# Row-maximum scores as three fp32r products of split queries and keys, and output weights loaded once per batch

## What is computed

```python
q = shape(query_states @ wq, T)          # B=8, T=128, D=512, 16 heads of 32
k = shape(key_value_states @ wk, S)      # S=2048
v = shape(key_value_states @ wv, S)
scores = jnp.einsum('bhtd,bhsd->bhts', q, k) + bias
weights = jax.nn.softmax(scores, axis=-1)
attn = jnp.einsum('bhts,bhsd->bhtd', weights, v)
attn = jnp.transpose(attn, (0, 2, 1, 3)).reshape(B, T, D)
x = x + attn @ wo
```

## Time and profile before

| | |
|---|---|
| median of 3 runs | 2052.88 us (2052.06 to 2055.56) |
| the profiled execution | 2055.39 us, of which 2053.6 us lie between its first and last instruction |
| PE busy | 1886.2 us, 92% of the span, 17102 matmul instructions |
| PEld, weight loads | 1431.3 us, 70% |
| DVE, ACT, POOL busy | 1130.7, 777.9, 804.0 us |
| mean granted TensorE clock | 0.959 of full speed |

### The profile page before, as it was taken

The page is one execution under the profiler, slowest core; times in us unless marked ns, Lnnn a source line. Parts: engine busy times, 40 slices in busy tenths (PEclk is TensorE's granted clock), DMA queues, the critical chain, the costliest instruction groups (busy, mean ns, idle before and its releaser), DMA issues. The chain is left out here.

```text
span 2053.6 us, 40698 instructions
## 1 busy us (share of the span) xinstructions
PE 1886.2 (92%) x17102; PEld 1431.3 (70%) x17102; DVE 1130.7 (55%) x2160; ACT 777.9 (38%) x1295; POOL 804.0 (39%) x641
## 2 busy tenths in 40 slices
PE   7599999999999999999999999579879998599995
PEld 3477777677677677677677777367657877499995
DVE  4244656656656556657556557464765233455553
ACT  1233434344344434344344334241244130355552
POOL 0114677668668677667667662000000000100001
PEclk9899999999999999999999999789989997699998
DMA  8622121121121122122122101210041004799993
GB/s 166 209 88 87 53 73 56 54 79 58 48 78 58 52 73 63 47 76 70 38 78 68 35 30 33 90 52 14 1 139 31 1 1 173 281 368 358 359 359 110
DMA packets 101126, 210.82 MB, mean 103 GB/s; under 512 B 9088, under 2 KB 33968, under 8 KB 95840
## 3 DMA queue, kind: packets, MB, share of 16 engines
q1 hardware_dynamic: 99488, 204.02, 29.4%
q0 software_dynamic: 1472, 4.40, 0.7%
HBM read 187.68 MB, written 20.71 MB: 101 GB/s over the span
## 5 line engine op out<-in xcount | busy, mean ns | idle before, releaser
L369 POOL TENSOR_TENSOR total<-total,probT 128x512 f32<-128x512 f32 x392 | 502.7, 1282 | 231.6 <-ACT probT L411 207.5
L488 DVE TENSOR_REDUCE negm<-bank 128x1 f32<-128x512 f32 x512 | 326.8, 685 | 179.4 <-PE bank L572 175.0
L469 DVE TENSOR_TENSOR probT<-bank,shift 128x512 f32<-128x512 f32 (+1 forms) x512 | 291.2, 615 | 216.2 <-PE bank L584 216.2
L411 ACT ACTIVATE probT<-probT 128x1024 f32<-128x1024 f32 x256 | 271.2, 1060 | 227.4 <-DVE probT L469 214.6
L405 ACT ACTIVATE v<-bank 128x512 f32<-128x512 f32 x128 | 76.4, 597 | 478.3 <-PE bank L552 478.3
L345 POOL TENSOR_TENSOR ctx_lo<-ctx_raw,ctx_hi 128x512 fp32r<-128x512 f32 x128 | 165.7, 1295 | 153.2 <-ACT ctx_hi L391 148.9
L552 PE MATMUL bank<-ctx_hi,wkv_hi 128*128 128x512 f32 x512 | 152.1, 419 | 22.5 <-ACT ctx_hi L391 22.5
L602 PEld LDWEIGHTS bank<-probT,v 128*32 128x32 f32 x4096 | 104.0, 109 | 94.0 <-ACT probT L411 92.0
L584 PEld LDWEIGHTS bank<-q,k 32*128 32x128 f32 x4096 | 126.0, 186 | 46.5 <-issue 44.1
L1348 POOL MEMSET zero_sb<- 128x512 f32 x1 | 0.5, 525 | 393.2 <-POOLq L1118 393.2
L552 PE MATMUL bank<-wkv_hi,ctx_hi 128*128 128x512 f32 x512 | 152.6, 420 | 0.0
(11 more groups left out here) (236 smaller groups left out, 2800.8 us busy)
## 6 DMA issues: line engine op xcount, KB each, us to landing
w_sb<-w SPq DMA_DIRECT2D x10, 4096.0 KB, 14.2
w_sb<-w SPq DMA_DIRECT2D x40, 1024.0 KB, 6.3
ctx_raw<-ctxT SPq DMA_DIRECT2D x128, 256.0 KB, 3.2
bias<-bias_scratch SPq DMA_DIRECT2D x32, 512.0 KB, 5.3
shift<-turned_bias SPq DMA_DIRECT2D x32, 512.0 KB, 5.1
slots<-zero_sb SPq DMA_DIRECT2D x17, 256.0 KB, 3.0
bias_scratch<-btab SPq DMA_DIRECT2D x1, 3072.0 KB, 34.2
down_w<-down SPq DMA_DIRECT2D x11, 256.0 KB, 2.6
```

Of the source, the lines that this page charges most:

```text
L369: pool.tensor_tensor(total[:, g], total[:, g], part, ALU.add).then_inc(add_step, 1)
L411: act.activation(pT[:, u % 2, j:j + 2], pT[:, u % 2, j:j + 2], ACT.Exp).then_inc(exp_done, 1)
L469: dve.tensor_tensor(pT[:, u % 2, j, i0:], sc[:, i0:], shift[:, g, j].unsqueeze(1).broadcast_to([P, ST - i0, T]), ALU.add).then_inc(shifted, 1)
L488: dve.tensor_reduce(negm[:, c, h:h + 1], sc[:], AX.X, ALU.max, negate=True).then_inc(max_done, 1)
```

## The change

The scores of `scores(a)` are made of three fp32r products instead of one fp32 product: queries and keys are split into a rounded high part and the rest, and high times high, low times high and high times low are accumulated in the same PSUM bank. The three products form three rounds over the four strips. All four ring banks are waited for before the first round. ACT makes the high part of the keys by a second copy out of `kv_bank`, after the plain copy and after a wait for the scores of the step before (one buffer); `kv_out` is signalled by this second copy alone. DVE makes the low part (`key_low`), after the maxima of its step. Queries are split in slots 14, 15, 0 and 1 of the step loop, one head group per step. The tile for `wo` is given up: `wo` lies in the two bias buffers and is loaded once per batch in slot 5, after the batch's last bias addition; output moves from slot 3 to slot 8, the store of the residual row from slot 4 to slot 10, and the bias loads of the next batch wait for the output. Some semaphores of `query_phase` are merged with others, with the same order of work.

```diff
-WO_STEP = 2 * LAG + 3
+WO_STEP = 2 * LAG + 8
+Q_STEP = LAG - 2
...
+        wo = bias[:].rearrange("p u j w -> p (u j w)").rearrange("p (g d) -> p g d", g=G)
...
+                    if i % G == 0 and i >= 3 * G:
+                        sp.wait_ge(wo_mm, i // G - 2)
...
-                sp.dma_start(wo[:], env["wo"].rearrange("(c p) n -> p c n", p=P)).then_inc(wo_in, 16)
...
-                    if a == 4 and b >= 2:
+                    if a == 5 and b >= 2:
+                        sp.wait_ge(biased, HG * G * min(b + 1, B))
+                        sp.dma_start(wo, env["wo"].rearrange("(c p) n -> p c n", p=P)).then_inc(wo_in, 16)
+                    if a == 10 and b >= 2:
                         sp.wait_ge(x_done, b - 1)
...
-                    act.activation(k[:, n % C, g, :], kv_bank[:], ACT.Copy).then_inc(kv_out, 1)
+                    act.activation(k[:, n % C, g, :], kv_bank[:], ACT.Copy)
+                    if t:
+                        act.wait_ge(s_mm, HG * t)
+                    act.activation(k_hi[:], kv_bank[:], ACT.Copy).then_inc(kv_out, 1)
...
+                    if b:
+                        act.wait_ge(s_mm, HG * (C * G * b - G + g + 1))
+                    act.activation(q_hi[:, g, :], q[:, b % 3, g, :], ACT.Copy).then_inc(q_hi_done, 1)
...
+                def key_low(t):
+                    dve.wait_ge(kv_out, 2 * t + 1)
+                    dve.tensor_tensor(k_lo[:], k[:, t // G % C, t % G, :], k_hi[:].bitcast(F32), ALU.subtract
+                                      ).then_inc(k_lo_done, 1)
...
+                    dve.tensor_tensor(q_lo[:, g, :], q[:, b % 3, g, :], q_hi[:, g, :].bitcast(F32), ALU.subtract
+                                      ).then_inc(q_lo_done, 1)
...
                     if 1 <= t <= LAST_T:
                         maxima(t - 1)
+                    if t < LAST_T:
+                        key_low(t)
...
-                    pe.wait_ge(kv_out, 2 * a + 1)
+                    if m % C == 0:
+                        pe.wait_ge(q_lo_done, b * G + g + 1)
+                    pe.wait_ge(k_lo_done, a + 1)
                     for j in range(HG):
                         ring_wait(RING_USER["s", HG * a + j])
-                        rows = slice(j * DH, (j + 1) * DH)
-                        pe.matmul(ring[ring_s(a, j)][:], q[rows, b % 3, g, :], k[rows, m % C, g, :],
-                                  start=True, stop=True).then_inc(s_mm, 1)
+                    for i, (qs, ks) in enumerate(((q_hi, k_hi), (q_lo, k_hi), (q_hi, k_lo))):
+                        for j in range(HG):
+                            rows = slice(j * DH, (j + 1) * DH)
+                            mm = pe.matmul(ring[ring_s(a, j)][:], qs[rows, g, :], ks[rows, :], start=(i == 0), stop=(i == 2))
+                            if i == 2:
+                                mm.then_inc(s_mm, 1)
...
-                    if b == 0:
-                        pe.wait_ge(wo_in, 16)
+                    pe.wait_ge(wo_in, 16 * min(b + 1, B - 1))
```

More of the change, by code:

```diff
@@ L152, in _ @@
                 for i in range(2 * DC):
-                    act.activation(wkv_hi[:, i, :], wkv_raw[:, i, :], ACT.Copy).then_inc(whi_done, 1)
+                    act.activation(wkv_hi[:, i, :], wkv_raw[:, i, :], ACT.Copy).then_inc(std_done, 1)
                 for k in range(1, 2 * G, 2):
@@ L173, in _ @@
                                       ALU.subtract, ALU.mult).then_inc(normed, 1)
[L175 to L178, removed]
+                dve.wait_ge(turned, 1)
+                dve.tensor_copy(last[:], bank[6][0:H, BL - 1:BL]).then_inc(normed, 1)
+                dve.wait_ge(normed, B + 1)
+                dve.tensor_scalar(btab[:], bank[6][0:H, 0:BL], last[:], None, ALU.subtract).then_inc(normed, 1)
                 for b in range(B):
-                    dve.wait_ge(turned, b + 1)
+                    dve.wait_ge(turned, b + 2)
                     dve.tensor_copy(xT[:, :, b * T:(b + 1) * T],
@@ L194, in _ @@
                 pe.wait_ge(consts_in, 48)
-                pe.matmul(bank[6][0:H, 0:BL], relb[:], onehot[:], start=True, stop=True).then_inc(bias_mm, 1)
+                pe.matmul(bank[6][0:H, 0:BL], relb[:], onehot[:], start=True, stop=True).then_inc(turned, 1)
                 for b in range(B):
@@ L232, in attention_phase @@
         v = sb("v", [P, C + 1, ST, D])
+        k_hi = sb("k_hi", [P, CS], F32R)
+        k_lo = sb("k_lo", [P, CS], F32R)
         q = sb("q", [P, 3, G, T])
+        q_hi = sb("q_hi", [P, G, T], F32R)
+        q_lo = sb("q_lo", [P, G, T], F32R)
         bias = sb("bias", [P, 2, HG, BW])
@@ L430, in _ @@
                     high_part(0, i)
+                for g in range(G):
+                    query_high(g)
                 for t in range(STEPS):
@@ L443, in _ @@
                         keep_shift(i // (C * G) * G + i % (C * G))
+                    i = t - Q_STEP
+                    if i >= 0 and i % (C * G) < G and i // (C * G) < B - 1:
+                        query_high((i // (C * G) + 1) * G + i % (C * G))
                     if t in TURN_AT:
@@ L511, in residual @@
                     dve.tensor_tensor(x_row[:], misc[:], x_row[:], ALU.add).then_inc(x_done, 1)
+                for g in range(G):
+                    query_low(g)
                 for t in range(STEPS):
@@ L517, in _ @@
                         maxima(t - 1)
+                    if t < LAST_T:
+                        key_low(t)
+                    i = t - Q_STEP
+                    if i >= 0 and i % (C * G) < G and i // (C * G) < B - 1:
+                        query_low((i // (C * G) + 1) * G + i % (C * G))
                     i = t - TOTAL_STEP
```

20 lines of the change are left out of this document (12 added, 8 removed).

## The result

The changed kernel takes 2056.68 us, median of 20 runs, against 2053.5 us of the kernel before beside it: ratio 1.0015 (95% interval 1.0008 to 1.0022), 3 us slower where 2044.2 was forecast (range 2035 to 2065). The profiled execution took 2057.82 us, 2056.0 of them in its span.

The account below looks back on a forecast made before the run. PE was taken as the bound, with other engines close behind. Seven batches at -0.86 (-6.0) and steps 1 to 15 (-2.7) gave -8.7 us, forecasting 2044.2 us against a median of 2052.9; range 2035 to 2065.

Parts of the forecast that it names:

- +0.13 a step in slots 14, 15 and 0: The denominators' sum waits for the shifts' copy, queued behind the keys' second copy: +0.13 a step instead of -0.18.
- the moved output, put at nothing: Output projection moved from slot 3 to 8: costs its 3.5 us there as before, so no net change.
- rival 4: Loads of the scores' later rounds don't hide; scores take 1.11 us, total 2064 us; chance 0.06.
- The scores: Three fp32r rounds of 0.227 us plus 0.21 make 0.89 instead of 1.07: 0.18 us saved a step.
- rival 5: An fp32r round costs an fp32 pass, 0.43 us; scores cost 1.50, total 2107 us; chance 0.11.
- The second copy, plain steps and slots 2 and 3: ACT's second copy of the keys is hidden by 0.06 us in plain steps; slots 2 and 3 cost +0.02 each.
- The low part: DVE's key subtraction waits for POOL's last addition in slot 4, so slot 5 costs +0.51 us instead of -0.18.
- Rival 1: The subtraction does not wait for POOL, slot 5 gains 0.18: 2039.4 us, or 2035.7 with cheaper rounds; chance 0.28.
- rival 3: A waiting subtraction never gets between POOL's additions; eleven more slots a batch make steps 0.69 late: 2097 us; chance 0.07.
- used three steps later: Splitting queries, four small pieces per batch on ACT and DVE, was put at nothing because they are used three steps later.
- The sum: -0.86 a batch, -6.0 for seven batches, and -2.7 for steps 1 to 15: together -8.7 us.
- Rival 2: Second copy cannot overlap the first's end as both read one bank, starting 0.58 later: 2051 us, no change; chance 0.12.

Follow-up runs that it names:

- seven: Changed kernel with low parts of keys and queries made by comparison with old PSUM scores (zeros), so one SBUF operand: 2051.22 us, ratio 0.9993.
- eight: Changed kernel with the last-but-one batch's output back in step 131 and the shifts' copy before the keys' second copy in slots 14, 15, 0: 2046.06 us.
- ten: Changed kernel, output and shifts' copy moved (step 131; slots 14, 15, 0), plus queries' low part between next step's shift and maxima: 2043.06 us, ratio 0.9945.
- five: Kernel before with only the output projection of every batch but the last moved from slot 3 to slot 8: 2057.08 us, ratio 1.0013.
- three: Changed kernel with ACT's copy of the shifts put ahead of the second copy of the keys in four slots: 2053.83 us, ratio 1.0000.
- one: Kernel before with only the scores' three fp32r rounds, no second copy or low parts, output in slot 3: 2034.38 us, ratio 0.9910.
- six: Changed kernel with the last load of the output weights issued only after POOL has added to the last shifts: 2055.43 us, ratio 1.0006.
- nine: Changed kernel, output back in step 131, shifts' copy first in slots 14, 15, 0, low parts by comparison with PSUM (zeros): 2037.79 us, ratio 0.9925.

## Why the prediction was wrong, point by point

Two terms of the sum failed: +0.13 a step in slots 14, 15 and 0 was too small, and the moved output, put at nothing, costs in the tail. That 2056.68 lies within the range of 2035 to 2065 owes nothing to the reasoning: the upper end came from rival 4, which falls.

- **The scores: right** (0.91 for 0.89; a plain step saves 0.16 for 0.18). The later rounds' loads hide and a round costs 0.23, so rivals 4 and 5 fall. Here the trace goes on disagreeing with the rule of the Trainium skill cited there (TensorE: Matmul & The Clock Gate, Part 3, The mechanism): twelve loads into four strips fit into 0.91 us, and those of the second round run under the products of the first.
- **The second copy, plain steps and slots 2 and 3: right** (+0.02 measured in slot 2). **Slots 14, 15 and 0: the mechanism was right, its size was not.** The term +0.13 measured +0.41, +0.41 and +0.52. I let the copy start 0.98 after the scores and the sum 0.05 after the copy of the shifts; they were 1.10 and 0.15, together 0.22 of the 0.28 missed in slot 15, and in slot 0 DVE's low parts come on top. The 0.05 was taken from another pair of lines, exponentials and mix; it holds again in slot 5 (838.71 to 838.76), and why the sum takes 0.15 is open. That is 0.95 a batch of the 1.00 missed; the 0.19 missed in the eight other slots and the 0.18 over-charged to slot 5 nearly cancel.
- **The low part: right in kind.** The subtraction is held up by POOL's fourth addition; slot 5 cost +0.33, not +0.51, since the next shift starts 0.47 after the addition's end and not 0.61. Rival 1 falls, and so does rival 3, since DVE gets in between two additions: in slot 15 its subtraction ends at 785.10, ahead of the end of POOL's four additions at 780.52 + 5.71 = 786.23. The rule of the Trainium skill cited there (SBUF — State Buffer, Who interferes with whom) fits these numbers: 892 and 1359 ns with both of DVE's operands in SBUF, 677 and 1284 with one in PSUM. But I looked for the wait only in slot 4. The query's low part was put down as hidden, "used three steps later", though the reciprocals stand behind it. What is used late can still delay what is queued behind: in the changed kernel the low parts of keys and queries together cost 0.11 in slot 0 beside the late sum (seven); in eight, where the sum is not late, moving the query's low part gives back 0.30 in slot 15 and 0.18 in slot 1 (ten).
- **"`output` costs its 3.5 us in slot 8 as in slot 3": wrong in the tail**, the costliest single step: it was put at nothing, the tail costs 4.6 us, and moving the output alone costs 3.3 there (five). In the batches the claim is true (3.43 against 3.43). After the last projection PE has little else, and the output in step 131 was the work under which POOL and DVE made the shifts. I named the cover for the loads, not for the work moved away.
- **The sum:** -6.0 for seven batches measured +1.0 (steps 16 to 127, of them 0.6 in step 16, where no mix covers the second copy), -2.7 for the first steps -2.35, and the tail 0 became +4.6. These are 11.9 of difference; 0.8 in the other direction before the first projection and behind step 142 leaves the 11.1 between the forecast -8.7 and the +2.4 between the two profiled spans. Rival 2 said no change, but its reason falls: the second copy does start 0.47 after the first (704.05 and 704.52 in slot 7), although both read one bank.

## What to carry to other kernels

Work added to an engine that is 40% or 60% busy must be followed through its queue: who stands behind it, in each kind of step, and who waits for that. When work is moved, ask what it was hiding where it stood, above all in the tail, where nothing else fills the engine. Of two things queued behind each other, put first the one that is waited for first, slot by slot.

## What the hardware showed that I had not expected

- After PE's wait at the end of step 131 the mean clock of step 132 was 0.66 (changed kernel, 2.43 us of waiting), 0.67 (five, 1.56), 0.50, which is 1.2 GHz throughout (three, 2.75), and 1.00, the upper level of 2.4 GHz (seven, 1.94). The length of the wait alone doesn't order them; what does, these runs don't show.
- The last 512 KB load of shifts took from 3.1 us (five) to 4.4 us (one) to land; in six it took 4.1, with the load of `wo` held back until it had landed.
- A DVE subtraction of 128 columns with both operands in SBUF took 0.28 us in one place of eight and 1.35 beside POOL's additions in another; with one operand in PSUM an instruction of that size took 0.28 beside POOL's additions too (nine).
